# First attention scores on 64 array rows, and the output bias added by GpSimd

## What is computed

```python
def _L0_...                      # context-query attention, then 8 experts, top 2
...
def _L1_xattn_ref(decoder_input, encoder_output, W_q, W_k, W_v, W_o, b_o):
    # HEADS = 16, HEAD_DIM = 8
    Q = (decoder_input @ W_q).reshape(B, Sd, HEADS, HEAD_DIM)
    K = (encoder_output @ W_k).reshape(B, Se, HEADS, HEAD_DIM)
    V = (encoder_output @ W_v).reshape(B, Se, HEADS, HEAD_DIM)
    scores = jnp.einsum('bqhd,bkhd->bhqk', Q, K) / jnp.sqrt(jnp.float32(HEAD_DIM))
    attn = jax.nn.softmax(scores, axis=-1)
    out = jnp.einsum('bhqk,bkhd->bqhd', attn, V).reshape(B, Sd, E)
    return out @ W_o + b_o
...
x = x + _L0_xattn_ref(_layernorm(x), ctx_1024, ...)
x = x + _L0_ffn_ref(_layernorm(x), ...)
x = x + _L1_xattn_ref(_layernorm(x), ctx_1024, W_q, W_k, W_v, W_o, b_o)
x = x + _L1_ffn_ref(_layernorm(x), ...)      # product in 8-bit float values
```

## Time and profile before

| | |
|---|---|
| Time, median of 3 runs | 243.28 us (242.24 to 243.68) |
| Span of the profiled execution | 241.2 us |
| TensorE busy | 200.3 us (83%), 1226 products |
| VectorE busy | 173.9 us (72%) |
| ScalarE busy | 139.8 us (58%) |
| POOL busy | 114.9 us (48%) |
| Weight loads busy (beside products) | 155.8 us (65%) |

### The profile page before, as it was taken

One profiled execution on the slowest core, in us unless ns is written; L12 is line 12 of the kernel. 1 busy time (PEld: TensorE's weight loads), 2 busy tenths in 40 slices (PEclk: granted clock), 3 DMA queues, 4 the chain that ended last, 5 costly groups with the idle time before them and its releaser, 6 DMA issues.

```text
span 241.2 us, 4289 instructions
## 1 busy us (share of the span) xinstructions
PE 200.3 (83%) x1226; PEld 155.8 (65%) x1226; DVE 173.9 (72%) x405; ACT 139.8 (58%) x265; POOL 114.9 (48%) x127
## 2 busy tenths in 40 slices
PE   5489989389398999999997688999999999886420
PEld 4377889165286888888885567777766877554210
DVE  2558366956956878878785899988979878735564
ACT  0268781316365475655557527898769777673442
POOL 3402263994357789898986523223223322203412
PEclk9979979959889999999999979999999999999655
DMA  7970400020043652464230000000000000000002
GB/s 234 427 309 1 174 4 0 0 90 0 0 134 143 209 195 91 152 217 143 108 97 0 0 0 0 3 5 0 0 3 0 0 0 0 4 0 0 0 3 87
DMA packets 8273, 17.08 MB, mean 71 GB/s; under 512 B 1209, under 2 KB 4026, under 8 KB 8002
## 3 DMA queue, kind: packets, MB, share of 16 engines
q1 hardware_dynamic: 6816, 16.03, 18.4%
q10 hardware_dynamic: 1442, 0.87, 1.1%
HBM read 10.04 MB, written 0.56 MB: 44 GB/s over the span
## 4 chain that ended last, share of the span: by engine, by line
PE 63%; DVE 17%; DMA 8%; ACT 4%; issue 4%; POOL 2%; ACTq 1%; SPq 0%; DVEq 0%; POOLq 0%
PE banks L1238 6%; PE bank L1219 6%; PE bank L1011 6%; PE bank L1012 6%; PE bank L1013 6%; PE bank L1250 5%; DMA wg<-in_wg 4%; PE banks L1011 4%; PE banks L1013 4%; PE banks L1012 4%; DVE xn L658 3%; DMA wxs<-wx 2%; DVE negm L877 2%; PE bank L1069 2%; PE bank L1272 2%
## 5 line engine op out<-in xcount | busy, mean ns | idle before, releaser
L298 POOL TENSOR_TENSOR hids<-attT,hids 128x512 fp32r<-128x512 f32 x32 | 40.7, 1294 | 17.2 <-ACT hids L480 17.2
L877 DVE TENSOR_REDUCE negm<-bank 128x2 f32<-128x512 f32 x64 | 42.1, 688 | 4.2 <-PE bank L1219 2.6
L340 POOL TENSOR_TENSOR wx<-raw,const 32x256 fp32r<-32x256 f32 x32 | 19.5, 610 | 43.8 <-DVE raw L867 37.0
L539 ACT ACTIVATE raw<-banks 128x1024 f32<-128x1024 f32 x32 | 32.5, 1022 | 2.6 <-PE banks L1238 2.3
L804 DVE SCALAR_TENSOR_TENSOR att<-att,bank 128x512 f32<-128x512 f32 x32 | 22.0, 688 | 16.2 <-ACT att L473 16.2
L473 ACT ACTIVATE att<-bank 128x512 f32<-128x512 f32 x32 | 19.1, 599 | 17.2 <-PE banks L1013 12.0
L1219 PE MATMUL bank<-wx 128*128 128x512 f32 x64 | 25.2, 436 | 2.2 <-DVE wx L887 1.2
L480 ACT CAST hids<-attT 128x512 fp32r<-128x512 f32 x32 | 19.7, 622 | 12.3 <-PE banks L1013 11.7
L1011 PE MATMUL bank<-xT,wxs 128*128 128x512 f32 x48 | 20.5, 428 | 0.8 <-DMA wxs<-wx 0.6
L1012 PE MATMUL bank<-xT,wxs 128*128 128x512 f32 x48 | 19.9, 415 | 0.0
L276 POOL TENSOR_TENSOR wx<-raw,wx 128x512 fp32r<-128x512 f32 x8 | 10.4, 1312 | 19.9 <-ACT wx L408 19.8
(11 more groups left out here) (215 smaller groups left out, 486.2 us busy)
## 6 DMA issues: line engine op xcount, KB each, us to landing
wxs<-wx SPq DMA_DIRECT2D x8, 512.0 KB, 4.7
rwb<-routing SPq DMA_DIRECT2D x8, 512.0 KB, 4.1
raw<-in_w SPq DMA_DIRECT2D x1, 2048.0 KB, 10.9
wxs<-wx SPq DMA_DIRECT2D x8, 256.0 KB, 4.2
raw<-in_w SPq DMA_DIRECT2D x1, 1024.0 KB, 13.6
xs<-in_x SPq DMA_DIRECT2D x1, 512.0 KB, 3.9
ctxT<-in_ctxT SPq DMA_DIRECT2D x1, 512.0 KB, 4.9
ctx<-in_ctx SPq DMA_DIRECT2D x1, 512.0 KB, 5.9
```

The costliest lines, as they stand in the source:

```text
L298: pool.tensor_tensor(hids[:, p, 1, k, :], hid[:, k, :], plain(hids[:, p, 0, k, :]), ALU.subtract).then_inc(S["hid_lo"], 1)
L340: pool.tensor_tensor(km[rows, g, j, :], ks[rows, g % 2, :], const[rows, C_ZERO:C_ZERO + 1].broadcast_to([QUAD, SEQ]), ALU.add)\
L539: act.activation(probs[:, g % 2, 2 * r:2 * r + 2, :, :].rearrange("p h k q -> p (h k q)"), pair[r][:, :], ACT.Exp, scale=ATT_SCALE).then_i ...
L877: dve.tensor_reduce(negm[:, g % 2, r // 2, c0:c0 + QUAD + 1:QUAD], bk[1 + r % 2][:, :].rearrange("p (h k) -> p h k", h=2), AX.X, ALU.max, ...
```

## The change

The first scores now contract over 64 rows: piece `r` takes rows 0 to 63 (heads 0 and 1 of the group) or 64 to 127 of both operands, and the product is placed on that half of the array's rows. Number and size of the outputs are as before. The output bias is no longer added by TensorE: `bo` is loaded to all 128 partitions, and POOL adds it to `xs` in two halves of 4 tiles, each after the third norm has read that half; `add_attention` waits for both. The row of ones and its memset go.

```diff
-        bo = sb("bo", [1, P])
-        ones = sb("ones", [1, P])
+        bo = sb("bo", [P, P])
...
-            pool.memset(ones[:, :], 1.0)
...
             values(0, True)
+            for h in range(2):
+                tiles = slice(*HALVES[h])
+                pool.wait_ge(S["ln3"], HALVES[h][1])
+                pool.tensor_tensor(xs[:, tiles, :], xs[:, tiles, :],
+                                   bo[:, :].unsqueeze(1).broadcast_to([P, TPH, P]), ALU.add)\
+                    .then_inc(S["bo_added"], 1)
+            pool.wait_ge(S["bo_added"], 2)
             pool_batch(0, True, False)
...
             def add_attention(b, tiles):
                 dve.wait_ge(S["wo_ps"], b + 1)
+                dve.wait_ge(S["bo_added"], 2)
...
                 t, pair = r // 2, r % 2
-                pe.matmul(bk[1 + r % 2][:, :], qs[:, g, t * P:(t + 1) * P],
-                          km[:, g, 2 * pair:2 * pair + 2, :].rearrange("p h k -> p (h k)"),
-                          start=True, stop=True).then_inc(S["s1_ps"], 1)
+                rows = slice(2 * QUAD * pair, 2 * QUAD * (pair + 1))
+                pe.matmul(bk[1 + r % 2][:, :], qs[rows, g, t * P:(t + 1) * P],
+                          km[rows, g, 2 * pair:2 * pair + 2, :].rearrange("p h k -> p (h k)"),
+                          start=True, stop=True, tile_position=(2 * QUAD * pair, 0)).then_inc(S["s1_ps"], 1)
...
                 for t in range(TPB):
-
-                    pe.matmul(bk[7][:, t * P:(t + 1) * P], ones[:, :], bo[:, :], start=True, stop=False)
                     ins = pe.matmul(bk[7][:, t * P:(t + 1) * P], aoT[:, t * P:(t + 1) * P], wo[:, :],
-                                    start=False, stop=True)
+                                    start=True, stop=True)
...
-        "wo": a["L1_xattn_W_o"], "bo": a["L1_xattn_b_o"].reshape(1, P), "fk": ...
+        "wo": a["L1_xattn_W_o"], "bo": rows(a["L1_xattn_b_o"]), "fk": ...
```

More of the change, by code:

```diff
@@ L188, in build @@
           hid_lo y_ps y_w y_acc accT_ps moe_s x3T_ps x3T_hi x3T_lo early_ps proj_ps q_hi k_hi qs_s ks_s km_act
-          km_pool s1_ps s1_max mT_ps qa_s s2_ps p_s v_s pv_ps o_ev oT_ps den_s ao_s aoT_ps aoT_ev wo_ps x3_s
+          km_pool s1_ps s1_max mT_ps qa_s s2_ps p_s v_s pv_ps o_ev oT_ps den_s bo_added ao_s aoT_ps aoT_ev wo_ps x3_s
           rs_s kv_s kovf_s fv_s q_s ovf_s f_s r_s r_pool q_pool nmr_s yz_pool out_pool xq_s fT_ps fT_ev f_ps y_s
@@ L1419 @@
         "wq": stacked(a["L1_xattn_W_q"]), "wk": stacked(a["L1_xattn_W_k"]), "wv": a["L1_xattn_W_v"],
-        "wo": a["L1_xattn_W_o"], "bo": a["L1_xattn_b_o"].reshape(1, P), "fk": a["L1_ffn_kernel"], "fb": rows(a["L1_ffn_bias"]),
+        "wo": a["L1_xattn_W_o"], "bo": rows(a["L1_xattn_b_o"]), "fk": a["L1_ffn_kernel"], "fb": rows(a["L1_ffn_bias"]),
     }
```

## The result

The changed kernel takes 255.87 us, the median of 4 runs (254.41 to 257.16), beside 243.25 us (median of 4) for the kernel before: a ratio of 1.057, 95% interval 1.048 to 1.066. It is slower by 12.6 us. The forecast was 250.6 us with a range up to 253.5, so the direction was right and the size was not: 5.3 us are missing in the sum. The profiled execution has a span of 254.2 us, 13.0 more than before.

What follows compares the result with a forecast made beforehand. TensorE was taken to bound the kernel, its delays paid nearly in full from about 145 to 217 us. Scores +11.3, bias -4.85, POOL +0.8 and entry +0.1 gave +7.35, so 250.6 us, range 244 to 253.5.

Steps and rivals of the forecast that it cites:

- The price of a change: TensorE switching between 64-row scores and full-array products: 0.20 us per change of array shape, bounds 0 and 0.20.
- lone piece: First-score piece 3 or 0, standing between full-array operations: two new changes of shape, +0.40 us each per group.
- Rival A: Halves of the array need no change of shape, so the kernel gets faster: 239.0 us, chance 0.12.
- rival C: A change to half an array costs half, 0.10 us: 244.1 us, chance 0.09.
- The pair side by side: First-score pieces 1 and 2 stream together on different halves: -0.12, then +0.20 for the change behind, together +0.07 us.
- rival B: The two halves run one after the other, 0.12 us more in about 12 groups: 252.1 us, chance 0.09.
- 0.87 us: Added time for one group's first scores in the loop: +0.07 for pieces 1 and 2, +0.40 each for 3 and 0.
- The bias: Output layers without the bias product on TensorE: -3.7 on the chain, -0.3 in waits, 0.85 gained in the tail; -4.85 us.
- POOL's additions: At the attention entry, POOL's first addition holds up VectorE's first normalisation: +0.8 us, bounds 0 and 1.3; second addition 0.
- rival D: The clock falls for one more half-clock stretch because of added waits: +1.7 us, 252.3 us, chance 0.05.

Runs made afterwards that it cites:

- both additions late: Changed kernel with scores on 128 rows and POOL waiting for all normalisations before its first addition; 239.37 us, ratio 0.989 to the kernel before.
- the bias alone: Changed kernel with first scores back on all 128 rows, so only the output bias is moved to POOL; 241.23 us, ratio 0.998 to the kernel before.
- ten changes: Changed kernel with scores on 128 rows and five unread 1-row products added in each group; 264.48 us, ratio 1.090 to the kernel before.
- scores alone: Kernel before with only the first scores on 64 rows, bias still a TensorE product; 259.42 us, ratio 1.077.
- six and ten changes: The six: changed kernel with scores on 128 rows and three unread 1-row products added in each group; 253.96 us, ratio 1.043 to the kernel before.
- the lone pieces alone: Changed kernel with only pieces 3 and 0 on 64 rows, pieces 1 and 2 on 128; 254.06 us, ratio 1.050 to the kernel before.

## Why the prediction was right in direction and too small

**The price of a change, 0.20 us: right for the 64-row scores.** The weight load behind a lone piece comes 0.42 us after its start, and the chain has 0.39 more for each lone piece and its successor. Rival A (no price) and rival C (half the price) are both refuted by it. The one-row products that were added are cheaper, at most 0.16 us a change, so the price is not one number for every part of the array. The Trainium skill (TensorEngine Tiling (Array Packing), Key Properties) puts the drain at a change of mode, not of the tile in it, and the trace agrees: four lone changes pay, and the two halves of the pair start 0.13 us apart (188.57 and 188.70) where a lone piece holds the next product back for 0.42.

**The pair side by side: right.** Two scores take 0.43 us in the chain together, where one alone takes 0.43, so rival B is refuted. The forecast term was +0.07; the chain shows -0.23 and +0.18, that is -0.05. With the 0.11 us that the transposes no longer wait, most groups cost 0.7 us instead of 0.87 (0.67 to 0.70 for groups 3 to 5, 0.47 to 0.87 in the loop where no output layer lies). This is most of the 1.9 us by which the stretch from group 2 to 15 was overrated.

**The bias: right.** 4.85 us was the term; with both additions late the traces show 4.4 us from group 7 on. The two output layers behind group 15, the tail's among them, give 1.8 of the forecast 2.1. In the tail the addition is bound by the conversion, as the working said.

**POOL's additions: mechanism right, price low.** The normalisations lose 0.43 us in the changed kernel and 0.72 in the bias alone, where +0.8 was taken. But the working priced only VectorE's loss. With the bias alone the delay goes with a stretch of 10.2 us at half clock instead of 3.4 and 1.1 us more in groups 0 and 1; when POOL waits, both are gone. The ratio moves by 0.009, some 2 us, with intervals that touch. The delay does not always bring the longer stretch: in the trace of ten changes the normalisations took 1.54 us, and the stretch was 3.4 us.

**The clock: the step that failed.** The sum has no term for the clock. Only rival D had it, at one more stretch of 3.4 us, +1.7 us, with a chance of 0.05, "against: with 0.87 us more in a group TensorE still streams most of the time". Three faults are in that. The sentence was taken from the steady groups of the loop; but the earlier trace rows show the clock at half while the first scores of group 0 are made, and groups 0 and 1 have no value products, so they are thinner than a group of the loop. It weighed how busy TensorE is, and TensorE is busy 94% in the stretch where the clock stays at half. And it took the end of the stretch as given at 142.8, as if the changed groups had no part in it. The term, measured: groups 0 and 1 take 15.4 us from second scores to second scores of group 2. At their old times and the forecast 0.87 each they would take 9.9. The **5.5 us** between them I put down to the clock. It is an estimate by subtraction, since no run has these groups on 64 rows at full clock. They are as much as the whole miss; the 1.9 too much for the later groups stands against 0.9 at the entry, part of which is at half clock too, 0.8 ahead of it and 0.3 in the tail.

What holds the clock is settled in part. It is not POOL (scores alone), not the empty place ahead of 139 us (filled), not the late groups. Scores on 64 rows at the entry and in the first groups do it, the lone ones above all, and full-array products in the same groups shorten it to 13.7 us. Gaps as such did not do it from 147 us on (six and ten changes); ahead of that they were not tried. Whether the chip counts the rows that work, or whether something else of a 64-row product matters, stays open: filling the idle half beside the lone pieces did not help, but it was filled for 256 columns of 512 only, and from group 1 on. The stretch also varies without a cause that these runs show: 3.4, 10.2 or 13.7 us among kernels with 128-row scores, and an early and a late return with the lone pieces alone. A single trace of 13.7 us is therefore weak evidence; for the full-array products the sums speak too, 44 to 45 us in all four runs against 50 to 56.

## What to carry to other kernels

A product on a part of the array between full-array products costs two changes of shape, here 0.20 us each for 64-row scores; put the parts side by side, or next to operations which have changed the shape anyway, or leave the full array in place though half of its rows are zeros. Where the trace shows the clock at half, price every edit behind that place for the case that it stays at half: look at which full-array work stands there, and not at the busy share. And where TensorE waits at such a place anyway, a few products to no purpose are worth a try: here they came to 0.007 of the time, which these runs do not tell from nothing.

## What the runs showed of the hardware that was not expected

- TensorE busy in 9.39 of 10 us was granted 0.50 of its clock when that work held 64-row scores and few products, and full clock with the same busy time on 128 rows. A busy share counts stretched products too, so it says nothing of the clock.
- At half clock a lone 64-row score with the projection behind it costs 1.23 us (0.72 and 0.51), at full clock 0.75; eight second scores behind the pair cost 2.00 and 1.14.
- A delay of 0.7 us on VectorE at the entry went with 6.8 us more at half clock in the profiled execution. In the time it went with about 2 us, by intervals that touch.
- With 128-row scores, nine full-array products without use at the entry went with no half clock there at all, and with the bias on POOL (both additions late) the kernel came to 0.98 of the time before. With 64-row scores the same nine left 20.5 us of it.
